# Indirect gathers placed one by one behind output adds, and the engines' expert loops turned one block later

## What is computed

```python
gates = softmax(xf @ Wg.T); topw, topi = top_k(gates, 2)      # 4096 tokens, 8 experts
C = int(round(2 * T * 1.05 / 8))                              # slots of an expert
buf[e, pos] = xf[token]                                       # tokens gathered by expert
h = gelu(einsum('ecd,edh->ech', buf, W1) + b1)
y = einsum('ech,ehd->ecd', h, W2) + b2
out[token] += topw * y[e, pos]                                # summed back by token
x = x + tanh(g_ffn) * out
```

## Time and profile before

| | |
|---|---|
| time before, median of 3 runs | 2054.86 us (2045.74 to 2057.12) |
| profiled execution, its own time | 2034.05 us |
| its span | 2032.3 us |
| PE matmul busy | 1859.9 us (92%) |
| DVE busy | 1277.3 us (63%) |
| ACT busy | 1108.0 us (55%) |
| POOL busy | 677.1 us (33%) |
| output adds (L674) | 288, 485.7 us of POOL |

### The profile page before, as it was taken

One profiled execution on the slowest core, in us unless ns is written; L12 is line 12 of the kernel. 1 busy time (PEld: TensorE's weight loads), 2 busy tenths in 40 slices (PEclk: granted clock), 3 DMA queues, 4 the chain that ended last, 5 costly groups with the idle time before them and its releaser, 6 DMA issues.

```text
span 2032.3 us, 34102 instructions
## 1 busy us (share of the span) xinstructions
PE 1859.9 (92%) x11068; PEld 1597.8 (79%) x11068; DVE 1277.3 (63%) x2881; ACT 1108.0 (55%) x2035; POOL 677.1 (33%) x506
## 2 busy tenths in 40 slices
PE   4989887689998999899999999899989998999997
PEld 3777765578887887788787878788878887888886
DVE  3698987676665665666475647565756575657652
ACT  2667666555554555455554546365645564556542
POOL 0000010434345333533343334433443334333333
PEclk8999987699999999999998999899989998999999
DMA  5264534425555555455545555555545554554544
GB/s 164 84 230 144 203 108 146 98 61 100 96 108 103 91 96 101 102 95 96 106 101 93 93 107 105 89 96 108 106 86 96 111 100 88 99 111 86 91 70 59
DMA packets 177809, 214.73 MB, mean 106 GB/s; under 512 B 20464, under 2 KB 102512, under 8 KB 176608
## 3 DMA queue, kind: packets, MB, share of 16 engines
q0 software_dynamic: 50176, 90.77, 30.4%
q1 hardware_dynamic: 127456, 121.74, 19.0%
HBM read 123.10 MB, written 89.34 MB: 105 GB/s over the span
## 4 chain that ended last, share of the span: by engine, by line
PE 80%; DVE 6%; issue 4%; ACT 3%; DMA 3%; another core or an unknown queue 3%; SPq 1%; POOL 0%; DVEq 0%; POOLq 0%; ACTq 0%
PE PS L980 37%; PE PS L958 31%; PE PS L805 3%; DMA vs<-in_ctx_dram 2%; PE PS L796 2%; PE PS L936 2%; PE PS L744 1%; PE PS L869 1%; SPq L452 1%; PE PS L824 1%; PE PS L758 1%; DVE h_lo L1703 1%; ACT heads L1087 1%; DVE y_out L1712 1%
## 5 line engine op out<-in xcount | busy, mean ns | idle before, releaser
L674 POOL DMA_INDIRECT out_dram<-y_out,rows_now x288 | 485.7, 1686 | 928.5 <-ACT y_out L1283 802.7
L958 PE MATMUL PS<-x_hi,w_hi 128*128 128x270 f32 x1792 | 525.6, 293 | 24.4 <-issue 13.2
L958 PE MATMUL PS<-x_lo,w_hi 128*128 128x270 f32 x1792 | 521.9, 291 | 8.8 <-issue 8.4
L958 PE MATMUL PS<-x_hi,w_lo 128*128 128x270 f32 x1792 | 520.7, 291 | 8.3 <-issue 8.1
L980 PE MATMUL PS<-w_hi,h_hi 128*120 128x512 f32 x1152 | 466.0, 405 | 39.8 <-DVE y_out L1712 18.6
L980 PE MATMUL PS<-w_hi,h_lo 128*120 128x512 f32 x1152 | 458.8, 398 | 0.8 <-issue 0.8
L980 PE MATMUL PS<-w_lo,h_hi 128*120 128x512 f32 x1152 | 459.1, 399 | 0.2 <-issue 0.2
L958 PEld LDWEIGHTS PS<-x_hi,w_hi 128*128 128x128 f32 x1792 | 344.0, 192 | 54.2 <-issue 22.5
L958 PEld LDWEIGHTS PS<-x_lo,w_hi 128*128 128x128 f32 x1792 | 344.5, 192 | 30.9 <-issue 9.4
L958 PEld LDWEIGHTS PS<-x_hi,w_lo 128*128 128x128 f32 x1792 | 343.3, 192 | 10.1 <-issue 10.1
L980 PEld LDWEIGHTS PS<-w_hi,h_hi 128*120 128x120 f32 x1152 | 212.0, 184 | 86.5 <-DVE y_out L1712 27.2
(11 more groups left out here) (192 smaller groups left out, 2289.6 us busy)
## 6 DMA issues: line engine op xcount, KB each, us to landing
w_raw<-in_L_ffn_W_dram SPq DMA_DIRECT2D x128, 256.0 KB, 3.4
w_raw<-in_L_ffn_W_dram SPq DMA_DIRECT2D x64, 512.0 KB
x_front<-in_x_dram SPq DMA_DIRECT2D x8, 1024.0 KB, 7.0
vs<-in_ctx_dram SPq DMA_DIRECT2D x32, 256.0 KB, 4.8
maxima<-maxima_rows SPq DMA_DIRECT2D x8, 1024.0 KB, 4.7
x_back<-in_x_dram SPq DMA_DIRECT2D x8, 1024.0 KB, 8.8
out_dram<-x_back SPq DMA_DIRECT2D x8, 1024.0 KB, 6.7
xn_rows<-xn SPq DMA_DIRECT2D x8, 1024.0 KB, 9.8
```

The source lines that it names most:

```text
L674: G.indirect_dma_start(out=out[:, :], out_offset=bass.IndirectOffsetOnAxis(ap=rows_now[0:RT, u % HI:u % HI + 1], axis=0), in_=y_out[0:RT, ...
L958: ins = T.matmul(product_at(k, i), w[:, slot, a, kt * P:(kt + 1) * P], v[:, side, x, kt, :], start=(kt == 0 and n == 0), stop=(kt == 1 and ...
```

## The change

POOL: the 14 gathers of block 3 are no longer one group. From block 4 on, one gather follows each output add until the 14 are out (block 10): first the five of side 0, then the nine of probabilities; the wait for `weight_copied` stands before the first of these nine. Of the five gathers of side 1, two stay at the end of block 14 and three go to block 15, each behind one output add. POOL's and SP's loops turn where they did.

PE, ACT and DVE: the body of an expert is cut into `step(e, k, ...)`. Ahead of the loop stand the 16 blocks of expert 0 and block 0 of expert 1; the loop's body is blocks 1 to 15 of expert e and block 0 of expert e + 1. The order of the blocks is the same.

DVE: the base of tile 0 moves from the start of block 3 to the end of block 2, and the base of tile 4 from before the M4 sum to behind it (`BASE_AT`); the first w2 split of a block moves from before the M4 sum to behind it. Ahead of expert 0, the second w1 pair is summed, rounded and split before the first rows are used, on DVE and ACT.

```diff
+        BASE_AT = {2: ((), (), (), (0,)), 3: ((), (1,), (2,), ()), 4: ((3,), (), (4,), ()),
+                   5: ((5,), (6,), (), ()), 6: ((7,), (8,), (), ())}
...
-            def gather_prob(rows):
-
-                for t in range(HI):
-                    G.indirect_dma_start(out=slot_prob[0:RT, t, :], out_offset=None, in_=prob_dram[:, :],
-                                         in_offset=bass.IndirectOffsetOnAxis(ap=rows[0:RT, t:t + 1], axis=0)
-                                         ).then_inc(prob_in, 16)
+            def gather_prob(rows, t):
+
+                G.indirect_dma_start(out=slot_prob[0:RT, t, :], out_offset=None, in_=prob_dram[:, :],
+                                     in_offset=bass.IndirectOffsetOnAxis(ap=rows[0:RT, t:t + 1], axis=0)
+                                     ).then_inc(prob_in, 16)
 
             gather_side(0, 0, slot_row, False)
             gather_side(0, 1, slot_row, True)
             pool.wait_ge(prob_stored, 32)
-            gather_prob(slot_row)
+            for t in range(HI):
+                gather_prob(slot_row, t)
+
+            def gather_next(e, n):
+
+
+                if n < 5:
+                    gather(rows_turn[:, TURNED[0][n]:TURNED[0][n] + 1], n, e * 10 + (5 + n + 1))
+                else:
+                    if n == 5:
+                        wait_apart(pool, weight_copied, e + 1)
+                    gather_prob(rows_turn, n - 5)
 
             def expert(e, first, last):
 
+                done = 0
                 for k in range(BLOCKS):
                     for u in scaled_in(k):
                         if not (first and u < 0):
                             add_rows(e, u)
+                        if 4 <= k < 14 and done < 5 + HI and not last:
+                            gather_next(e, done)
+                            done += 1
+                        if k == 15 and not last:
+                            s = 2 + u - 3 * HI
+                            gather(rows_turn[:, TURNED[1][s]:TURNED[1][s] + 1], s, e * 10 + (10 + s + 1))
                     if k == 2:
                         if not first:
                             for r in range(RINGS):
@@ -705,11 +725,10 @@
                         wait_apart(pool, prob_in, e * (16 * HI) + 16 * HI)
                         G.tensor_copy(rows_turn[:, :], slot_row[:, bass.ds(e * HI + HI, HI)]).then_inc(turn_rows_copied, 1)
                         wait_apart(pool, turn_rows_copied, e + 1)
-                        gather_side(e + 1, 0, rows_turn, True)
-                        wait_apart(pool, weight_copied, e + 1)
-                        gather_prob(rows_turn)
                     if k == 14 and not last:
-                        gather_side(e + 1, 1, rows_turn, True)
+                        for s in range(2):
+                            gather(rows_turn[:, TURNED[1][s]:TURNED[1][s] + 1], s, e * 10 + (10 + s + 1))
+                assert last or done == 5 + HI
...
+            for k in range(BLOCKS):
+                step(0, k, True, False)
+            step(1, 0, False, False)
             with pe.Fori(1, E - 1) as e:
-                expert(e, False, False)
-            expert(E - 1, False, True)
+                for k in range(1, BLOCKS):
+                    step(e, k, False, False)
+                step(e + 1, 0, False, False)
+            for k in range(1, BLOCKS):
+                step(E - 1, k, False, True)
...
             upper_w1(0, 0, 0)
-            for s in range(5):
+            take_rows(0, 0, 0)
+            take_rows(0, 0, 1)
+            upper_w1(0, 0, 1)
+            for s in range(2, 5):
                 take_rows(0, 0, s)
             for i in range(7):
                 upper_x(0, 0, i)
-            upper_w1(0, 0, 1)
-            expert(0, True, False)
+            for k in range(BLOCKS):
...
+                for u in middle:
+                    base_rows(e, u)
+                add_product(e, k, M4, c_rows[:, 0, :], c_rows[:, 0, :])
+
+                for d, p in w1s:
+                    split_w1(e + d, p, 1)
+                for u in late:
+                    base_rows(e, u)
+                for d, p in w2s[:1]:
+                    split_w2(e + d, p)
...
+                for u in end:
+                    base_rows(e, u)
...
             sum_w1(0, 0)
             for n in range(3):
                 split_w1(0, 0, n)
+            sum_w1(0, 1)
+            for n in range(3):
+                split_w1(0, 1, n)
             for p in range(2):
                 dve.wait_ge(x1_stored[p], START + 16 * (B // 2))
             dve.wait_ge(pad_stored, 16 * N_PAD)
@@ -1794,13 +1827,15 @@
                 sum_x(0, 0, n)
...
```

More of the change, by code:

```diff
@@ L983, in second_layer @@
                     ins.then_inc(y_tile, 1)
[L985 to L1014, removed]
@@ L1016, in _, with step, rows, rest @@
-            expert(0, True, False)
-            with pe.Fori(1, E - 1) as e:
-                expert(e, False, False)
-            expert(E - 1, False, True)
+            def step(e, k, first, last):
+                mine = [[q for q in part if not (first and q < 0)] for part in items(k)]
+                turn = (e, 1) if k == 0 else (e + 1, 0) if k == 14 and not last else None
+                def rows(s):
+                    if turn is not None:
+                        turn_rows(*turn, s)
+                def rest(part):
+                    for q in mine[part]:
+                        second_layer(e, q)
+                product(e, k, M1)
+                product(e, k, M6)
+                rows(0)
+                rest(0)
+                rows(1)
+                product(e, k, M7)
+                product(e, k, M5)
+                rows(2)
+                rest(1)
+                product(e, k, M4)
+                rows(3)
+                rest(2)
+                rows(4)
+                product(e, k, M3)
+                product(e, k, M2)
+                rest(3)
@@ new lines, in step @@
+            def step(e, k, first, last):
+                ys = [u for u in scaled_in(k) if not (first and u < 0)]
+                turn = (e, 1) if k in (0, 1) else (e + 1, 0) if k in (14, 15) and not last else None
+                copy_first(e, k)
+                if k == 0:
+                    wait_past(act, h_upper, e * NH_UP)
+                    A.copy(b1_now[:, :], b1_all[:, bass.ds(e * HT, HT)]).then_inc(b1_copied, 1)
+                    act.wait_ge(b1_copied, e + 1)
+                if k == 3:
+                    act.wait_ge(prob_in, e * (16 * HI) + 16 * HI)
+                    wait_past(act, y_ready, e * NY)
+                    A.copy(weight_now[0:RT, :], slot_prob[0:RT, :, bass.ds(e, 1)].rearrange("p t o -> p (t o)"))\
+                        .then_inc(weight_copied, 1)
+                    act.wait_ge(weight_copied, e + 1)
+                if turn is not None and k % 2 == 0:
+                    for s in range(5):
+                        take_rows(*turn, s)
+                        if s % 2 == 0 and s // 2 < len(ys):
+                            scale_rows(e, ys[s // 2])
+                else:
+                    for u in ys[:1]:
@@ L1321, in expert @@
                         scale_rows(e, u)
-                    for d, p in w2s[1:]:
-                        upper_w2(e + d, p)
-                    gelu_top(e, k)
                     if turn is not None:
-                        for i in ((0,) if k % 2 == 0 else (5, 6)):
+                        for i in range(1, 5):
                             upper_x(*turn, i)
+                    for d, p in wanted(SPLIT_W1, k, last):
+                        upper_w1(e, e + d, p)
+                    for u in ys[1:2]:
+                        scale_rows(e, u)
@@ L1329, in _ @@
+                w2s = wanted(SPLIT_W2, k, last)
+                for d, p in w2s[:1]:
+                    upper_w2(e + d, p)
+                gelu_rows(e, k)
+                for u in ys[2:]:
+                    scale_rows(e, u)
+                for d, p in w2s[1:]:
+                    upper_w2(e + d, p)
+                gelu_top(e, k)
+                if turn is not None:
+                    for i in ((0,) if k % 2 == 0 else (5, 6)):
+                        upper_x(*turn, i)
             upper_w1(0, 0, 0)
-            for s in range(5):
+            take_rows(0, 0, 0)
```

161 lines of the change are left out of this document (62 added, 99 removed).

## The result

The median is 1942.05 us (1937.9 to 1945.26, four runs). The kernel before, run beside it, has 2050.72 (2045.74 to 2057.12). The ratio is 0.947, interval 0.943 to 0.951. The profiled execution took 1937.90 us against 2034.05: 96.2 us less, where the sum of the prediction had 89.8. Between the medians it is 108.7 us less. The forecast of 1965 was thus 23 us too high, and the time lies at the low end of the range.

What follows compares the result with a forecast made beforehand. PE, busy 92% of the span, was taken as the bound, with time winnable only where it idles or runs at low clock. 2034.05 - 70 - 14.3 - 3.7 - 1.8 = 1944.3, plus 20.8 makes 1965 us; range 1942 to 2008.

Steps and rivals of the forecast that it cites:

- (a): Blocks 4 and 5 of each expert: spreading POOL's burst of 14 gathers ends the engines' starvation, -70 us.
- residue of 0.9 us per expert: Loss assumed to remain per expert after the gathers are spread, 6.3 us in all, set against -76.3.
- (b): Loop turn of PE, ACT and DVE moved one block later, between blocks 0 and 1: -14.3 us.
- the price of DVE's lag: At the moved turn, the h split at the start of block 2 comes late: 5 x 0.5 us.
- (c): First output base done at the end of block 2, ending PE's wait in block 3 of each expert: -3.7 us.
- (d): Last three side 1 gathers in block 15, each behind its add: in time with 1.7 us margin, 0 us.
- (e): Before expert 0, second w1 pair summed and split before the rows arrive, ending PE's wait in block 0: -1.8 us.
- 20.8 more: Distance from the profiled execution, 2034.05 us, to the median of the runs shown, 2054.86, added unchanged at the end.
- Half starvation: Rival: half the starvation stays near some gathers, blocks 6 to 10; -38 instead of -76, 2003 us; chance 0.16.
- another cause: Rival: the starvation does not come from the burst and spreading the gathers brings nothing; 2035 us; chance 0.07.
- late gathers: Rival: side 1 gathers in block 15 come late, stall and low clock seven times, 35 us; 2000 us; chance 0.05.
- a toll on single gathers: Rival: each of 98 lone gathers costs all engines 1.3 us, 127 in place of 76; 2100 us, slower; chance 0.05.

Runs made afterwards that it cites:

- POOL's order alone: Kernel before with only POOL's new gather order (gathers spread, side 1's last three in block 15): 1962.3 us against 2048.02, ratio 0.959.
- all but the spread: Changed kernel with POOL's old order put back (14 gathers at the end of block 3, 5 at the end of block 14): 2031.61 us, ratio 0.992.
- old turn: Changed kernel with the loops of PE, ACT and DVE turned between blocks 15 and 0 again: 1955.86 us, ratio 0.956.
- first run spread: Changed kernel with the nine probability gathers ahead of expert 0 spread over its first three blocks: 1941.32 us, ratio 0.948.
- the nine at block 3: Changed kernel with nine probability gathers in one go at the end of block 3, row gathers single from block 4: loop 1559.6 us, one execution.
- nine at block 8: Changed kernel with an expert's nine probability gathers in one go at the end of block 8, row gathers single: loop 1515.7 us, one execution.

## Why the prediction was right or wrong

**(a), the cause and the place: right.** The marks went to 23.0 in every expert, and POOL's order alone brings it (-76.6 of the loop). **Its residue of 0.9 us per expert: wrong**, 6.3 us too much; no block near a single gather is longer, and leaving 63 of them out wins nothing. I took the 0.0 to 0.9 us behind the five in a run for the price of gathers that stand alone. The five of block 14, two now and three single, gave another 2.3 that had not been counted.

The rule of the Trainium skill that spoke against it (DMA: Bandwidth & Descriptors, "SWDGE vs HWDGE vs iDMA") does not decide: ratio 0.959 for the order alone, 88.5 us back without it. It speaks of a DMA engine's queues, and those were 6% busy while PE starved, so it may hold and yet say nothing of what the other engines lost.

**(b): right**, -14.1 by the marks and -14.4 by the experiment, for -14.3; that it agrees to some tenths is luck, as the turns scatter by 3 us and more from one execution to the next. (The 24.3 us that it starts from are 24.0 with the exit's 37.47.) Part of the gain is the clock: behind mark 15 it fell to between 0.70 and 0.76 over 5 us at three of the five old turns, and it stays at 1.00 for the 40 us there in all five after. The step that chose the price of DVE's lag, 0.5 us in block 2, was not the real course: mark 0 to 1 is 12.9 to 13.4 at a turn and 10.3 to 10.5 without, so the loss lies in block 1, where PE's gap stands, DVE's overlaps it, and block 2 gives some of it back (1.5 to 2.4 us a turn remain). DVE's gap is shorter than counted (2.3 to 2.8 us in the kernel after, not 4.0). That the turn's gap cannot be hidden but only placed was right for PE. The rule of the Trainium skill quoted there (Runtime: NRT & Kernel Launch, "Instruction fetch mechanics") agrees: without a taken branch the gap is 0 (mark 15 to 2 is 37.5 in every expert with the loops written out).

**(c): mechanism right, mis-sized**, 5.0 us for 3.7. The base's wait of 0.44 to 0.51 us is not all that block 3 gains (0.7 to 0.8 us); which of DVE's other reorderings gives the rest was not tried apart.

**(d): right.** The last side 1 gather of that turn is issued at 960.34, PE turns the rows in block 0 without a wait for a DMA.

```profile
960.34 1.20 POOL L666 DMA_INDIRECT gathered<-xn_rows,rows_turn  x1 [0.30 <-issue]
```

**(e): wrong**, 0 for -1.8: mark 0 is at 404.4 before and 404.6 after, and from the first row gather it is 32.8 us before and 33.4 after. PE's wait for the first products' sums went, but a 3.2 us wait for ACT stands beside block 0, which now runs into the first run of gathers. The earlier trace rows had been read for DVE alone; that the first run "costs the others little" does not follow from it, and the runs with it spread show 2.2 to 4.0 us.

Against the profiled execution these make -6.3, -2.3 and +2 for (a), -0.1 for (b), -1.3 for (c), +1.8 for (e) and -0.2 that lies outside the loop or in rounding, -6.4 us in all: 1944.3 becomes 1937.9, as measured.

**The step that failed is the last: "20.8 more, and I add that at the end unchanged".** After, the median lies 4.2 us above the profiled execution, not 20.8; that is 16.6 of the 23 us. The 20.8 us were no fixed cost of an unprofiled run. They were the distance from one profiled execution to the median of three other runs, 2054.86; a fourth run brought that median to 2050.72, which is 4.1 of them. Other runs of the same kernel have other distances:

| kernel | run of 14 in it | runs, and their range in us | median, us | median less its profiled execution |
|---|---|---|---|---|
| before, first session | yes | 4, 11.4 | 2050.7 | 16.7 |
| before, three later sessions | yes | 10, 14.4; 7, 6.9; 9, 15.5 | 2048.0; 2049.2; 2035.1 | 14.0; 15.1; 1.0 |
| all but the spread | yes | 7, 13.9 | 2031.6 | 6.8 |
| POOL's order alone | no | 4, 2.6 | 1962.3 | -0.7 |
| old turn | no | 4, 5.1 | 1955.9 | 1.5 |
| after | no | 4, 7.4 | 1942.05 | 4.2 |
| first run spread | no | 4, 5.1 | 1941.3 | 3.3 |
| loops written out; with first run spread | no | 4, 2.3; 5, 6.5 | 1930.2; 1929.8 | -1.5; 1.4 |

A single run in one more session gave 2030.7 for the kernel before. The four later sessions ran on four different chips. So the kernel before moved by 13 to 20 us from one session to another, and its profiled 2034.05 is the level of the two sessions with the shorter times; the kernel with loops written out, with a small edit besides, moved by 0.4. Without the run of 14 the distance is -1.5 to 4.2. This suggests that the extra time belonged to the very stalls that were removed, but it does not show it: there is no trace of a slow execution of the kernel before, the ranges of kernels with and without the run overlap (6.9 and 7.4), and with the stalls put back the distance was 6.8, not 12 to 20. What is shown is that the distance did not carry over. The prediction had this in its range ("if the unprofiled runs lose more at these places"), but only as its edge of 1942. With 4.2 in place of 20.8 the sum would have been 1948.5.

**The rivals.** Half starvation, another cause, late gathers, a toll on single gathers: none came; the toll of 1.0 us a gather is measured at 0 for the 63 of probabilities. (The half case takes -38 off -76, while the sum carries -70; by the sum it is 1997, not 2003.) What came was one that wasn't listed: that more goes than the profile shows.

**What stays open.** That a run of nine or more small gathers starves PE, ACT and DVE is shown; how is not. Much of the time is lost at no semaphore. A long run of row gathers alone, or of output adds, was not tried, so whether the kind of transfer matters is open too. Two queues carry instructions. The records of the one with the larger transfers show them 17 to 25 us apart in quiet stretches and 31 us apart around the run of the kernel before (1051.5 to 1082.8, with the run from 1050.7 to 1068.6) and 27 around the nine at block 3 (1040.8 to 1067.9). That would fit instructions held up behind the gathers; an engine that stands still for another reason would ask for its next instructions later too, so the longer distance may be what follows from the stall. With nine at block 8 it is 27 as well (1077.7 to 1104.9), with hardly a loss, so the delay alone doesn't explain the price. Work in hand when the run begins, how soon each engine next needs instructions, and the row gathers that follow the run at block 3 would fit with both; none was tried alone.

## What to carry to other kernels

In a kernel like this one, gathers that POOL issues belong one by one, or in runs of at most five (the longest that was cheap in every place tried), behind instructions that POOL issues anyway; look for them wherever several engines stand idle at once with "issue" or "remote" inside work that has no semaphore. Let the loops of all engines turn at one place, where what the slowest one delivers is wanted latest, or write them out. When an edit removes stalls whose length isn't explained, don't carry the distance between profile and median over: it may be part of them. And take that distance, and any edge of a range, from more than one session of the same kernel.

## What was not expected of the hardware

- Nine gathers of 120 rows by 32 bytes, 1.3 us apart, cost 0.0 to 8.8 us, by place and by what else differed there; fourteen cost 6.8 to 12.5, five 0 to 1.0, one alone nothing.
- PE keeps its pace for 9 to 13 us into a run and is slow till some us behind its end (three matmuls from 1070 to 1075, behind the run that ends at 1068.6); the clock of 0.50 comes last, when PE has been waiting, and adds to the price.
- A turn of the loop leaves DVE idle for 2.2 to 4.5 us and PE for 1.0 to 2.5; the program with all loops written out (30359 instructions in its trace) had no such gap and showed no price of its own.
